# A decoder of six sublayers: the last batch of its first self attention written apart, with the experts' weight splits placed among its heads and its output sent tile by tile

## The reference, cut to what matters

```
x = x + L0_attn(layernorm(x))       # 16 heads of 32, rotary positions, softmax, output product
x = x + L0_xattn(layernorm(x), itok, ctx, ctx, ctx)
    # four experts, one for each token by its token id; expert e has
    # Wg = Wu = Wd = ctx[e]:  y = (silu(h @ W.T) * (h @ W.T)) @ W.T
x = x + L0_ffn(layernorm(x))        # 1-bit MLP
x = x + L1_attn(layernorm(x))       # self attention without rotation
x = x + L1_xattn(layernorm(x), ctx, mask)
x = x + L1_ffn(layernorm(x))        # fp8 linear
```

## Time and profile before

| | |
|---|---|
| time, median of 3 runs | 1781.85 us (1776.4 to 1787.78) |
| the profiled execution, own time | 1790.49 us |
| its span, first to last instruction | 1788.6 us |
| mean granted TensorE clock | 0.934 of full speed |
| TensorE busy | 1509.2 us (84%) |
| VectorE busy | 1259.1 us (70%) |
| ScalarE busy | 888.4 us (50%) |
| GpSimd busy | 552.8 us (31%) |

### The profile page before, as it was taken

One profiled execution on the slowest core, in us unless ns is written; L12 is line 12 of the kernel. 1 busy time (PEld: TensorE's weight loads), 2 busy tenths in 40 slices (PEclk: granted clock), 3 DMA queues, 4 the chain that ended last, 5 costly groups with the idle time before them and its releaser, 6 DMA issues.

```text
span 1788.6 us, 27098 instructions
## 1 busy us (share of the span) xinstructions
PE 1509.2 (84%) x8774; PEld 585.6 (33%) x8775; DVE 1259.1 (70%) x1768; ACT 888.4 (50%) x1081; POOL 552.8 (31%) x448
## 2 busy tenths in 40 slices
PE   1789999999848993788688999999979999999928
PEld 1223323233226661344332323333222333323213
DVE  4587897878845556888367788787736777768675
ACT  1336272452622333788645546463746454554634
POOL 0535447453420004422232232323132232414120
PEclk9889999999969997899888999999989999999969
DMA  3710202102123446200030111102231120203002
GB/s 117 246 37 3 70 25 60 34 15 56 63 101 107 141 135 142 36 1 0 6 108 18 39 34 27 45 13 58 94 98 45 36 59 23 70 9 85 0 30 95
DMA packets 80861, 106.32 MB, mean 59 GB/s; under 512 B 14112, under 2 KB 51360, under 8 KB 80672
## 3 DMA queue, kind: packets, MB, share of 16 engines
q1 hardware_dynamic: 77216, 97.14, 18.5%
q0 software_dynamic: 3584, 8.39, 2.2%
HBM read 49.26 MB, written 18.35 MB: 38 GB/s over the span
## 4 chain that ended last, share of the span: by engine, by line
PE 40%; DVE 9%; issue 5%; ACT 5%; DMA 2%; POOL 1%; POOLq 0%; SPq 0%; DVEq 0%; ACTq 0%
PE ps L426 16%; PE ps L805 6%; PE ps L972 5%; PE ps L819 5%; PE ps L1872 2%; ACT arena L1113 2%; PE ps L1854 2%; DVE arena L1165 1%; PE ps L750 1%; PE ps L2188 1%; PE ps L776 1%; DVE arena L1405 1%; DVE stats L180 1%; DVE arena L2026 1%; DMA x<-sorted_y,place 1%
## 5 line engine op out<-in xcount | busy, mean ns | idle before, releaser
L1113 ACT ACTIVATE arena<-ps 128x1024 f32<-128x1024 f32 x384 | 372.8, 1024 | 118.2 <-PE ps L972 107.4
L1165 DVE TENSOR_REDUCE arena<-ps 128x2 f32<-128x1024 f32 x256 | 299.6, 1220 | 58.0 <-PE ps L750 57.8
L426 PE MATMUL ps<-xt,w 128*128 128x512 f16 (+1 forms) x1872 | 304.1, 313 | 19.8 <-DVEq L152 8.8
L805 PE MATMUL ps<-arena 128*32 128x512 f32 x1536 | 210.6, 621 | 14.8 <-DVE arena L1200 8.8
L972 PE MATMUL ps<-arena 97*128 97x512 f16 (+1 forms) x768 | 214.7, 395 | 9.6 <-ACT arena L1113 6.8
L426 PEld LDWEIGHTS ps<-xt,w 128*128 128x128 f16 (+1 forms) x1872 | 153.6, 100 | 161.5 <-issue 58.8
L426 PE MATMUL ps<-w,arena 128*128 128x512 f16 (+1 forms) x804 | 185.9, 381 | 12.6 <-issue 12.6
L1326 DVE TENSOR_TENSOR arena<-arena 128x1024 f32<-128x1024 f32 x128 | 173.6, 1396 | 13.4 <-PE ps L819 11.8
L1535 POOL TENSOR_TENSOR arena<-arena 128x512 f16<-128x512 f32 x96 | 115.9, 1209 | 168.8 <-ACT arena L1093 164.0
L1088 ACT ACTIVATE arena<-ps,arena 128x512 f32<-128x512 f32 x96 | 65.8, 687 | 182.8 <-PE ps L426 175.4
L1405 DVE TENSOR_SCALAR arena<-arena 128x1024 f32<-128x1024 f32 x128 | 106.7, 839 | 69.4 <-ACT arena L1113 68.7
(11 more groups left out here) (200 smaller groups left out, 2029.7 us busy)
## 6 DMA issues: line engine op xcount, KB each, us to landing
arena<-arena SPq DMA_DIRECT2D x576, 64.0 KB, 2.0
raw<-in_ctxT SPq DMA_DIRECT2D x8, 1024.0 KB, 5.6
raw<-in_ffn_parts SPq DMA_DIRECT2D x16, 512.0 KB, 3.6
sorted_x<-arena SPq DMA_DIRECT2D x1, 4864.0 KB, 27.4
arena<-sorted_x SPq DMA_DIRECT2D x19, 256.0 KB, 3.5
sorted_y<-arena SPq DMA_DIRECT2D x19, 256.0 KB, 2.1
out<-x SPq DMA_DIRECT2D x16, 256.0 KB, 2.0
x<-in_x SPq DMA_DIRECT2D x1, 3072.0 KB, 15.8
```

What stands on the lines that cost most here:

```text
L426: last = pe.matmul(out, left[l](cl[k]), right[r](cr[k]), start=start and k == 0 and a == 0, stop=stop and k == n - 1 and a == 2)
L805: last = pe.matmul(self.context(g)[HD * j:HD * (j + 1)], self.v[:, kb, HD * (HG * g + j):HD * (HG * g + j + 1)], self.p(u)[:, j * S:(j + 1 ...
L1113: act.activation(self.p(u)[:, 2 * h * S:(2 * h + 2) * S], flat(self.m.ps[:, 2 * h:2 * h + 2, :]), ACT.Exp, scale=SOFTMAX_SCALE).then_inc(s ...
L1165: v.tensor_reduce(self.mx[:, g % 2, j:j + 2, t:t + 1].rearrange("p h t -> p (h t)"), self.slot_banks(item, b), AX.X, ALU.max).then_inc(sel ...
```

## The change

Batch 3 of attn0 is taken out of the loops (they run over 1 and 2) and written with a constant b. In it:

- the norm, the transposes and the copies for a "next" batch are left out (plan without "x");
- SP issues the weights' first load as soon as it has issued the batch's last stacking transfer, the second after `sent` of batch 2, the third when the values' product has read xt, the fourth when the first is split; GpSimd gives `sent` before the low parts;
- ScalarE splits weight k after the exponentials of unit SPLIT[k] = 9, 11, 13, VectorE two units later, after its pair addition; the fourth on ScalarE after the output product, on VectorE after the last send was issued (`sent` counts NB now);
- the output product goes by tiles: chunks 0 to 2 of tiles 0 and 1, their chunk 3, then tiles 2 and 3 whole (pe_last_out);
- VectorE takes for each tile the addition, statistics and combining, and applies the norm of the tile before (dve_last_out); GpSimd makes a root for each tile and sends each tile by itself, with its own carrier (pool_tile, pool_send).

```diff
+    def pool_tile(self, g, b, i):
+        m = self.m
+        g.wait_ge(*self.at(self.moments, b * T + i + 1))
+        g.tensor_tensor(m.rstd[:, i:i + 1], m.mv[:, i, 1:2], m.eps[:, 0:1], ALU.add).then_inc(self.eps_added, 1)
+        g.wait_ge(*self.at(self.eps_added, b + i + 1))
+        g.tensor_tensor(m.rstd[:, i:i + 1], m.rstd[:, i:i + 1], m.mhalf[:, 0:1], ALU.pow).then_inc(self.rstd_ready, 1)
+    def dve_tile_stats(self, v, b, i, src):
+        m = self.m
+        self.dve_stats(v, src, (i,))
+        v.wait_ge(*self.at(self.sums, b * T + i + 1))
+        v.memset(m.carrier[:], 0.0)
+        v.bn_aggr(m.mv[:, i, :], m.stats[:, i, :]).then_inc(self.moments, 1)
...
         if self.rope:
-            sp.wait_ge(*self.at(self.slot_free[0], self.slot_count(0, NB)))
+
+            weights = self.following.weights
+            weights.load(sp, 0)
             sp.wait_ge(*self.at(self.sent, NB - 1))
-        self.sp_following(sp)
-        if self.rope:
-            self.following.weights.sp_rest(sp)
+            weights.load(sp, 1)
+            self.wait_full(sp, ("v", T - 1), NB - 1)
+            weights.load(sp, 2)
+            weights.sp_rest(sp)
+        else:
+            self.sp_following(sp)
...
+    def pe_last_out(self, pe):
+
+        pe.wait_ge(*self.at(self.cl, NB * C - 1))
+        for i in range(2):
+            self.pe_out(pe, i, range(C - 1))
+        pe.wait_ge(*self.at(self.cl, NB * C))
+        for i in range(2):
+            self.pe_out(pe, i, [C - 1]).then_inc(self.out_full, 1)
+        for i in range(2, T):
+            self.pe_out(pe, i, range(C)).then_inc(self.out_full, 1)
...
         if self.rope:
-            for n in range(NE - 1):
-                self.following.weights.act(act, n)
             act.wait_ge(*self.at(self.out_full, NB * T))
             self.following.weights.act(act, NE - 1)
...
+            if self.of_last(b) and u in self.SPLIT:
+                self.following.weights.act(act, self.SPLIT.index(u))
...
+    def dve_last_out(self, v, b):
+
+        src, dst = (lambda i: slot(self.m.x, b * T + i)), (lambda i: self.normed_tokens(b)[:, i, :])
+        self.dve_places(v, b)
+        for i in range(T):
+            self.dve_out(v, i, b)
+            v.wait_ge(*self.at(self.out_added, b * T + i + 1))
+            self.ynorm.dve_tile_stats(v, b, i, src)
+            if i:
+                self.ynorm.dve_tile_apply(v, b, i - 1, src, dst)
+        self.ynorm.dve_tile_apply(v, b, T - 1, src, dst)
+        v.wait_ge(*self.at(self.sent, NB))
+        self.following.weights.dve(v, NE - 1)
...
-            if u == (3 if self.rope else 0):
+            if self.of_last(b):
+                if u - 2 in self.SPLIT:
+                    self.following.weights.dve(v, self.SPLIT.index(u - 2))
+            elif u == (3 if self.rope else 0):
...
         if self.rope:
-            self.ynorm.pool(g, NB - 1)
-            self.pool_scatter(g, NB - 1)
+            self.pool_self(g, NB - 1, False)
+            for i in range(T):
+                self.ynorm.pool_tile(g, NB - 1, i)
+                if i:
+                    self.pool_send(g, NB - 1, i - 1, i)
+            self.pool_send(g, NB - 1, T - 1, T)
+            g.sem_inc(self.sent, 1)
             g.wait_ge(self.scattered, NB * (16 * T))
...
+        if self.of_last(b):
+            self.pool_sent(g, b)
         for c in range(C - 1):
             self.pool_context_low(g, c, b)
-        if self.rope and not first:
-            g.wait_ge(self.scattered, b * (16 * T))
-            g.sem_inc(self.sent, 1)
+        if self.rope and not first and not self.of_last(b):
+            self.pool_sent(g, b)
```

More of the change, by code:

```diff
@@ L610, with make_plan @@
     CROSS_WITH_UNIT = {12: ",,,x", 13: ",,,x", 14: ",,,x", 15: ",,,x"}
-    def make_plan(self, first):
+    def make_plan(self, first, last=False):
         out = ()
@@ L624, in make_plan @@
             out = () if first else self.WITH_OUT
+        if last:
+            units = {u: kinds.replace("x", "") for u, kinds in units.items()}
         places = [((name, n, step), k) for name, table in (("proj", proj), ("out", out), ("v", values))
@@ L918, in pe_project_values @@
             self.wait_free(pe, item, b)
-            if not self.cross and not isinstance(b, int):
+            if not self.cross and not first_of(b):
                 pe.wait_ge(*self.at(self.out_free, (b - 1) * T + i + 1))
@@ L998, in act_wait_chunks @@
     def act_wait_chunks(self, act, n, b):
-        if n < 2 and not self.cross and not isinstance(b, int):
+        if n < 2 and not self.cross and not first_of(b):
             if n == 0:
@@ L1248, in dve, with dve_places @@
         self.dve_batch(v, 0)
-        with v.Fori(1, NB) as b:
+        with v.Fori(1, NB - self.rope) as b:
             self.dve_batch(v, b)
+        if self.rope:
+            self.dve_batch(v, NB - 1)
         self.dve_context(v, C - 1, NB - 1)
         self.dve_last_low(v, NB - 1)
+        if self.rope:
+            self.dve_last_out(v, NB - 1)
+            return
         for i in range(T):
             self.dve_out(v, i, NB - 1)
-        if self.rope:
-            self.dve_final_moments(v, NB - 1)
-            self.dve_final_apply(v, NB - 1)
-            for n in range(NE):
-                self.following.weights.dve(v, n)
-        else:
-            self.following.dve_ahead(v)
+        self.following.dve_ahead(v)
+    def dve_last_out(self, v, b):
[10 more added lines that the diff above has]
+        self.following.weights.dve(v, NE - 1)
+    def dve_places(self, v, b):
+        v.wait_ge(*self.at(self.sent, b))
+        v.tensor_copy(self.place_now, self.m.place[:, bass.ds(b * T, T)]).then_inc(self.place_ready, 1)
     def dve_cross_batch(self, v, b):
@@ L1347, in dve_self_heads @@
                 self.norm.dve_stats(v, own, (0, 1))
-            if u == (4 if self.rope else 0):
+            if u == (4 if self.rope else 0) and not self.of_last(b):
                 self.norm.dve_stats(v, own, (2, 3))
@@ L1356, in dve_self_heads @@
             for i in range(T):
-                if u == (6, 6, 8, 8)[i] if self.rope else u == (4, 4, 6, 6)[i]:
+                if not self.of_last(b) and u == ((6, 6, 8, 8) if self.rope else (4, 4, 6, 6))[i]:
                     self.norm.dve_apply(v, b, own, lambda i: m.xn[:, i, :], [i])
@@ L1473, in pool_self @@
         if self.rope and not first:
-            self.norm.pool(g, b)
+            if not self.of_last(b):
+                self.norm.pool(g, b)
             self.pool_bias(g, self.ob, b)
```

75 lines of the change are left out of this document (49 added, 26 removed).

## The result

The changed kernel takes 1772.24 us (median of 10 runs, 1760.86 to 1773.87), the kernel before in the same comparison 1783.89 (10 runs, 1776.4 to 1791.4): a ratio of 0.9926, 95% interval 0.9909 to 0.9944. The forecast was 1770 with a range of 1762 to 1779. The profiled execution of the changed kernel has a span of 1770.4 us and took 1772.22.

A forecast was written before the change was run, and what follows sets the result against it. It took a serial stretch of 23 us after the output product as the cost to cut, with TensorE narrowly leading the heads. Tail gain 14.5 less 2.6 in heads and hand-over gave 11.9: 1781.85 to 1770 us, range 1762 to 1779.

The forecast's parts named there:

- A: The forecast case: the tail gains 14.5 us, heads and hand-over lose 2.6, giving 1770 us; chance 0.62.
- The tail: From the output product's end to the last send's end: 14.5 us gained, bounds 13.1 and 15.
- The last send ends at 506.8: End of GpSimd's sends after the output product: at 506.8 instead of 521.26, some 5.6 us after the last output matmul.
- The fourth split now waits on VectorE for the last send: After the sends: the fourth weight split, 2.29 us, runs under the last send's landing and costs 0 us.
- carriers under 0.5: Sign that the forecast is right: GpSimd's one-column carrier instructions at the end each take under 0.5 us.
- Without it addition 5 begins earlier; I take those 1.5 us (bounds 0 and 2.5).: In the heads: without the next batch's norm, VectorE's pair addition 5 starts 1.5 us earlier, at 473.0 instead of 474.49.
- addition 7 ending 1 to 2 us later: Sign that the forecast is right: VectorE's last pair addition ends 1 to 2 us later, counted from the heads' start.
- These 16.8 us: In the heads: VectorE's time from addition 5's start to addition 7's end with two splits, ending at 489.8 against 488.2.
- Rival B: In the heads: VectorE takes the lead, three splits paid in full, 6.9 us; gain 7.6, time 1774; chance 0.18.
- The hand-over: From the heads to the output product: 1.0 us lost, bounds 0 and 2, partly by GpSimd's low part being held.
- The clock (E): Heads and output product: gaps keep TensorE's clock low, costing 22.5 us; 10.6 slower overall, 1792 us; chance 0.04.
- The peeled batch: Last batch written outside each engine's loop: same instructions, 0 us, with bounds of -0.5 and +1.

The follow-up runs named there:

- The guard: Changed kernel with the signal releasing the fourth weight split given by a one-column GpSimd instruction behind the last send, not by the queue: 1766.98 us, ratio 0.9916.
- second profile: The changed kernel run and profiled again with no edit: 1767.87 us, ratio 0.9927.
- The spread kernel: Changed kernel with batch 3's four GpSimd bias additions each waiting for another of additions 2 to 5, and an earlier `sent` of batch 2: 1765.34 us, ratio 0.9902.
- spread and guard: Changed kernel with both the bias additions one by one and the last-send signal given by a GpSimd instruction: 1765.34 us, ratio 0.9894.

## Why the prediction was right, and where its steps were not

The time came out 2 us from the forecast, in the case taken as likeliest (A). The sum in place did not repeat: the load goes out 7.2 us earlier in one profile and 14.0 in the other, mean 10.6, against a forecast of 11.9. So the total is right with terms that were wrong in opposite directions and in part by chance of order. In the first pair of profiles, 18.2 us apart, the place of the change holds only 7.2; 1.4 stand ahead of the heads and 9.7 behind the load, where before's first profile was long by chance.

**The tail, 14.5 forecast, 12.7 measured.** The rows were read rightly: the stall was a stall, and the root of one column takes 0.57 as taken from the earlier trace rows. The term was mis-sized by 1.8 us: "The last send ends at 506.8" meant 5.6 us after the product, and it is 7.36. The guard shows 1.31 of it: "The fourth split now waits on VectorE for the last send" was wrong, it waited for GpSimd's queue. The other 0.5 is GpSimd's own queue, the step which took the moments of tile 3 as its only release; the rows 507.0 against 507.60 show that but no kernel tested it. One carrier of 1.51 us also missed the sign "carriers under 0.5". The 3.17 us to the load came out at 3.18, and the split under them cost nothing.

**"Without it addition 5 begins earlier; I take those 1.5 us (bounds 0 and 2.5)."** This step failed in both orders: 1.7 us later in one profile, 3.6 earlier in the other. It counted what VectorE and TensorE lose with the norm, and left out the queue that the norm's root stood in. With the root gone, GpSimd's bias additions move forward: in the first profile from 20.25 us after the heads' start to 18.32, so that they start ahead of addition 2 instead of behind it. In the second profile the held carrier pushes them back to 20.41, and addition 2 is free. The spread kernel shows what that costs. The sign "addition 7 ending 1 to 2 us later" failed with it: it ends 4.0 later in one profile and 1.2 earlier in the other.

**"These 16.8 us"** from addition 5 to addition 7 were measured at 16.06 with the splits in (before: 13.72). This held, and with it the reading that two splits are paid there. Rival B, the splits paid in full, overstates it: 3.5 us in the heads without the clock, not 6.9.

**The hand-over, 1.0 forecast, 1.5 or 0 measured.** The low part that was feared to be starved slipped between the two halves of addition 7 and took 1.40 us (488.41), ahead of split 2. The Trainium skill (SBUF — State Buffer, Who interferes with whom) has whichever starts first hold the shared port for its whole instruction. By that the low part would wait for one VectorE instruction at most, and this row agrees; the first half of addition 2 doesn't, which was held from 455.45 over three bias additions and took 4.76 us. What was lost at the hand-over was clock: from the end of addition 7 to the end of the product it is 14.44 us in the first profile against 12.97 before, and 12.95 in the second.

**The clock (E).** The mechanism exists, in small: in the first profile, after an idle of 3.90 us, the product had 0.84, and it cost 1.5 us, not 22.5. In the second the same idle of 3.90 stood ahead of a product of 11.03 us at 0.95, so the idle alone doesn't decide it. The late stretch 480.8 to 490.9 had 0.96.

**The peeled batch, 0 with bounds of -0.5 and +1.** In place it is +0.6. By time it may be a gain of 3 to 6 us; and all later kernels gained by the ratio some 4 to 7 us more than their load moved (guard: 15.0 against 10.75; spread and guard: 18.9 against 14.4). Part of the rest can be placed. The heads of the changed kernels start 0.2 to 3.7 us earlier than before's; and from the load to the end all eleven other profiles take 1250.1 to 1254.5 us, where before has 1264.2 and 1251.3. The profile with 1251.3 is a quick execution of before, 1777.86 us against a median of 1781.95. It may be that most executions of before lose some us there; two profiles of it don't show that, and no run shows why.

## What to carry to other kernels

When an instruction is taken out, read each queue that it stood in: what follows moves forward and meets something else, and a forecast needs the new neighbours, above all on engines off the critical path. Between VectorE and GpSimd, instructions in a row on one engine can hold one instruction of the other over several of them; here it went so in some traces and not in others, and spreading the row took the risk away. Where a semaphore is to mean that an engine has finished, let an instruction of that engine give it. Before two profiles are compared, check that they agree ahead of the edit: one program had two orders.

## What was not expected of the hardware

- The stall works both ways. A one-column GpSimd instruction took 6.58 us beside three splits of 2.28 to 2.29 in a row on VectorE, and VectorE's addition took 5.89 us instead of 2.31 beside four GpSimd additions of 1.24 each in a row. But a row is not enough for it: beside the same four additions it took 3.40 us in the kernel before and 3.61 in the second profile, where the engines took turns. What decides between the two was not found.
- An increment given by GpSimd's queue came before the engine's queued carrier and send: the split that it released started at 509.19, the send ended at 512.69. Given by an instruction, it came 0.02 us after the send (509.33 against 508.31 + 1.00).
- The same program ran in two orders, 5.3 us apart at the end of the heads. They part where TensorE's granted clock falls early (0.55) or late (1.00 in the same stretch), and differ first in the start of addition 1, by 0.9 us. That the clock decides it was read from thirteen traces, not tested.
